# Sorting the edges by source on chip, and summing equal sources by a scan in place of joining products and accumulating scatters

## The reference

```python
def L0(x, src, dst, w):                       # first layer
    agg = segment_sum(x[src] * w[:, None], dst)
    out = leaky(x * agg @ W1 + b1) + leaky(agg @ W2 + b2)
    return out / norm(out)
def L1(x, src, dst, w):                       # second layer
    nbr = x[dst]                              # neighbours are now the destinations
    m = gelu(gelu(nbr @ W1p + b1p) @ W2p + b2p) * w[:, None]
    agg = segment_sum(m, src)                 # summed at the sources
    out = gelu(gelu([x, agg] @ W1u + b1u) @ W2u + b2u)
    return out / norm(out)
x = layernorm(x + L0(x, ...))
x = layernorm(x + L1(x, ...))
```

## Time and profile before

| What | us |
|---|---|
| median of 3 runs | 2925.66 (2924.0 to 2927.83) |
| the profiled execution's own time | 2925.36 |
| its span | 2923.6 |
| stage 1, to its last scatter's start | 1254.2 |
| stage 2, first gather to last scatter's start | 1258.3 to 2535.5 |
| stage 3 | 2539.0 to 2923.6 |
| busy: PE / DVE / ACT / POOL | 2133.4 / 2219.9 / 1060.2 / 2327.0 |
| moved by DMA | 516.39 MB |

### The profile page before, as it was taken

One profiled execution on the slowest core, in us unless ns is written; L12 is line 12 of the kernel. 1 busy time (PEld: TensorE's weight loads), 2 busy tenths in 40 slices (PEclk: granted clock), 3 DMA queues, 4 the chain that ended last, 5 costly groups with the idle time before them and its releaser, 6 DMA issues. The chain is left out here.

```text
span 2923.6 us, 40992 instructions
## 1 busy us (share of the span) xinstructions
PE 2133.4 (73%) x12594; PEld 1674.9 (57%) x12594; DVE 2219.9 (76%) x5824; ACT 1060.2 (36%) x1964; POOL 2327.0 (80%) x1770
## 2 busy tenths in 40 slices
PE   3036555555555553369999999999998999699997
PEld 3035555555555543347777777777776666466664
DVE  5069988888888886547788777777777777278998
ACT  0000000000000000035555555545554555289997
POOL 7777888888888888758878888888888887479998
PEclk8555555555555555579999999999999999699998
DMA  9889888888888767568777777777776776456664
GB/s 227 214 197 200 178 177 180 175 178 183 180 183 172 160 142 155 96 163 183 185 185 184 180 167 181 181 169 175 179 181 157 184 172 149 89 173 219 222 219 169
DMA packets 1035280, 516.39 MB, mean 177 GB/s; under 512 B 539713, under 2 KB 997489, under 8 KB 1035065
## 3 DMA queue, kind: packets, MB, share of 16 engines
q1 hardware_dynamic: 764616, 372.57, 48.1%
q0 software_dynamic: 143440, 76.97, 19.0%
q10 hardware_dynamic: 127008, 64.23, 7.6%
HBM read 269.84 MB, written 243.78 MB: 176 GB/s over the span
## 5 line engine op out<-in xcount | busy, mean ns | idle before, releaser
L304 PE MATMUL sums<-xg,weigh 128*128 128x64 f32 x1960 | 431.8, 416 | 518.2 <-ACT ms L327 350.9
L557 POOL DMA_INDIRECT state<-ms,sidx x391 | 621.5, 1590 | 147.4 <-issue 117.4
L304 PEld LDWEIGHTS sums<-xg,weigh 128*128 128x128 f32 x1960 | 417.6, 325 | 551.2 <-issue 474.9
L260 POOL DMA_INDIRECT table<-ms,sidx x391 | 615.7, 1575 | 136.1 <-issue 114.7
L372 DVE TENSOR_SCALAR weigh<-rowp,key,ew 128x128 f32<-128x128 f32 (+3 forms) x784 | 424.2, 604 | 162.8 <-PE rowp L292 155.4
L538 POOL DMA_INDIRECT box<-table,node_dst x391 | 385.8, 987 | 126.6 <-issue 111.2
L247 POOL DMA_INDIRECT xg<-in_x,node_src x391 | 380.8, 974 | 120.7 <-issue 107.1
L327 ACT ACTIVATE ms<-sums 128x256 f32<-128x256 f32 x98 | 37.6, 384 | 1137.9 <-DMA table<-ms,sidx 996.8
L378 DVE SCALAR_TENSOR_TENSOR seen<-rowp,key,earlier 128x128 f32<-128x128 f32 (+3 forms) x784 | 383.6, 546 | 0.0
L588 PE MATMUL z_p<-turned_s,wz 128*128 128x512 f32 x588 | 326.9, 639 | 22.7 <-ACT turned_s L670 21.0
L598 PE MATMUL o_p<-cenz,leaky 128*128 128x65 f32 x2352 | 302.1, 288 | 42.0 <-DVE leaky L758 41.9
(11 more groups left out here) (97 smaller groups left out, 3555.2 us busy)
## 6 DMA issues: line engine op xcount, KB each, us to landing
box<-table SPq DMA_DIRECT2D x97, 768.0 KB, 5.2
joins<-weigh ACTq DMA_DIRECT2D x98, 640.0 KB, 3.8
weigh_in<-joins SPq DMA_DIRECT2D x98, 640.0 KB, 7.1
table<-rows SPq DMA_DIRECT2D x97, 512.0 KB, 5.3
pair<-state SPq DMA_DIRECT2D x97, 512.0 KB, 4.0
xin<-in_x SPq DMA_DIRECT2D x97, 256.0 KB, 6.1
state<-y SPq DMA_DIRECT2D x97, 256.0 KB, 7.5
out<-y SPq DMA_DIRECT2D x97, 256.0 KB, 2.2
```

Source lines behind the costliest of these rows:

```text
L260: pool.indirect_dma_start(out=table[:, :], out_offset=bass.IndirectOffsetOnAxis(ap=sidx[0][:, i:i + 1], axis=0), in_=ms[k % MR][:, b, :], ...
L304: last = pe.matmul(sums[k % 2][:, a * D:(a + 1) * D], block_of(0, k, b)[:, a * P:(a + 1) * P], xg[:, k * WT + b, :], start=b == a, stop=b ...
L557: pool.indirect_dma_start(out=state[:, :], out_offset=bass.IndirectOffsetOnAxis(ap=sidx[1][:, at:at + 1], axis=0), in_=ms[k % SM][:, b, :] ...
```

## The change

What it does:

- The second call of `equal_rows` (sources as keys), `store_join`, the tensor `joins` and its load are gone.
- Beside stage 1 the 50,000 edges (padded to 65,536 as 128 x 512) are sorted by source with a bitonic network: 136 compare-and-swap steps, 16 changes of sign and 14 transpositions (steps over partitions are made after PE has turned the 128 x 512 arrays). A swap step is a comparison (256 elements a partition), a copy by ACT and two predicated copies by DVE (768 elements a partition each). 48 of these 166 entries stand in windows 0 to 3, the others, one or two a window, up to window 83.
- In stage 2 the gathers and scatters follow the sorted order. After the second GELU, DVE multiplies with the weights (`weight`) and sums runs of equal source by a scan along the free dimension (`sum_runs`), whose start is the last column of the window before. PE turns the sums back (`turn_back`), ACT copies them, and POOL scatters them plainly: only the last edge of a run goes to a real row, the others each to a row of their own that nobody reads. The sorted list lies as two halves in the two halves of the partitions; one accumulating scatter at the end (`add_seam`) adds the run that crosses from one to the other.
- The scatters no longer wait for the window before, and `leak` no longer waits for `begun`.
- The bias of the second product is added by ACT, and the two products with 128 columns and the one with `ones` become one with 256 columns.

```diff
@@ first_edges, DVE: one swap step
+ def compare(phase, bit, done, before_it):
+     wait(dve, arranged, done)
+     wait(dve, laid, 3 * before_it)
...
+     dve.tensor_tensor(compact(above[:, 0:COLS // 2]..., bit)[:, 0, :, :],
+                       keys[:, 0, :, 0, :], keys[:, 0, :, 1, :], ALU.is_gt).then_inc(compared, 1)
+ def swap(phase, bit):
...
+     dve.wait_ge(compared, n + 1)
+     dve.wait_ge(kept, n + 1)
+     dve.copy_predicated(both[:, :, :, 0, :], mask, both[:, :, :, 1, :]).then_inc(lowered, 1)
+     dve.wait_ge(lowered, n + 1)
+     dve.copy_predicated(both[:, :, :, 1, :], mask, compact(lower[:, :, :], bit)).then_inc(arranged, 1)
@@ first_edges, DVE: the order per window
- for n, k in order:
-     equal_rows(n, k)
-     if n == 0:
-         scatter_rows(k)
-         if k < NCH:
-             build(k)
+ for k in range(NWIN):
+     part = 0
+     for kind, phase, bit, done, before_it in sorting(k):
+         if kind == "sign":
+             change_sign(phase, done, before_it)
+         if kind == "swap":
+             compare(phase, bit, done, before_it)
+             if part == 0:
+                 weigh_rows(k)
+             if part == 1:
+                 count_rows(k)
+                 scatter_rows(k)
+             part += 1
+             swap(phase, bit)
...
+     if k < NCH:
+         build(k)
@@ first_edges, ACT
- def store_join(w):
-     act.wait_ge(weighed, turn[1, w] + 1)
-     act.dma_start(joins[w]..., weigh[1][w % 2]...).then_inc(joined[w % 2], 16)
+ def keep_lower(phase, bit, done, before_it):
+     wait(act, arranged, done)
+     wait(act, laid, 3 * before_it)
+     act.activation(compact(lower[:, :, :], bit), pairs(edges[:, :, :], bit)[:, :, :, 0, :], ACT.Copy).then_inc(kept, 1)
@@ second_edges, SP
- def load_join(i):
-     wait(sp, summed, i - SW + 1)
-     sp.dma_start(weigh[i % SW]..., joins[i]...).then_inc(joined[i % SW], 16)
+ def load_runs(i):
+     wait(sp, summed, i - SW + 1)
+     for h in range(2):
+         at = (HALF * h + 2 * i) * P
+         sp.dma_start(run[i % SW][h * D:(h + 1) * D, :, :],
+                      runs[:, at:at + 2 * P]....to_broadcast([D, 2, 2 * P])).then_inc(joined[i % SW], 16)
@@ second_edges, POOL
+ def scatter(k):
+     pool.wait_ge(taken, k + 1)
+     for b in range(min(WT, FILLED - k * WT)):
+         of = column_of(HALF * (b % 2) + 2 * k + b // 2)
+         pool.indirect_dma_start(out=state[:, :], out_offset=...sorted_sidx[:, of:of + 1]...,
+                                 in_=ms[k % SM][:, b, :], in_offset=None).then_inc(scattered[k % SM], 16)
@@ second_edges, PE
- pe.matmul(ffo[:, 0:WT * D], ones[:, :], bp2[:, :], start=True, stop=False)
- for q in range(2):
-     last = pe.matmul(ffo[:, q * P:(q + 1) * P], g1[:, q * P:(q + 1) * P], wp2[:, :], start=False, stop=q == 1)
+ pe.matmul(ffo[:, 0:2 * P], wp2[:, :], g1[:, :], start=True, stop=True).then_inc(mixed2, 1)
+ def turn_back(i):
+     pe.wait_ge(summed, i + 1)
+     wait(pe, taken, i)
+     for j in range(2):
+         last = pe.transpose(ffo[:, (2 + j) * P:(3 + j) * P], total[i % 2][:, j * P:(j + 1) * P], ident[:, :])
+     last.then_inc(turned_back, 1)
...
  of(t, 2, products, 2)
- of(t, 5, join)
  of(t, 4, turn_neighbours)
  of(t, 2, outputs, 0)
+ of(t, 5, turn_back)
  of(t, 2, outputs, 1)
@@ second_edges, ACT: take stands later
  of(t, 2, slope, 2)
- of(t, 5, take)
  of(t, 3, square_centred)
  of(t, 4, neighbours_in)
+ of(t, 5, take)
  of(t, 2, square)
@@ second_edges, DVE
- if q == 2:
-     wait(dve, begun, i - 4)
+ def weight(i):
+     dve.wait_ge(gelu2, i + 1)
+     dve.wait_ge(joined[i % SW], 32 * (i // SW + 1))
+     dve.tensor_tensor(g2[i % 2][:, :], g2[i % 2][:, :], run[i % SW][:, 1, :], ALU.mult).then_inc(weighted, 1)
+ def sum_runs(i):
+     dve.wait_ge(weighted, i + 1)
+     wait(dve, summed, i)
+     wait(dve, turned_back, i - 1)
+     dve.tensor_tensor_scan(total[i % 2][:, :], run[i % SW][:, 0, :], g2[i % 2][:, :],
+                            total[(i - 1) % 2][:, 2 * P - 1:2 * P] if i else 0.0, ALU.mult, ALU.add).then_inc(summed, 1)
...
  for t in range(ROUNDS):
+     of(t, 5, weight)
+     of(t, 5, sum_runs)
      of(t, 2, sum_outputs)
```

More of the change, by code:

```diff
@@ L56, in gnn_kernel, with column_of @@
     BEFORE_SCATTER = 3
-    SPAN = ((1, 2, 3, 4), tuple(b % JOIN + 1 for b in range(WT)))
-    JW = sum(SPAN[1])
+    SPAN = (1, 2, 3, 4)
+    HALF = TILES // 2
+    assert TILES % 8 == 0 and E < P * COLS and N < PAST_ALL
+    def column_of(tile):
+        return tile % 4 * P + tile // 4
     table = nc.dram_tensor("table", (3 * N + PAD, D), F32, kind="Internal").ap()
-    state = nc.dram_tensor("state", (2 * N + PAD, D), F32, kind="Internal").ap()
-    joins = nc.dram_tensor("joins", (NWIN, JW, P, P), F32, kind="Internal").ap()
+    state = nc.dram_tensor("state", (2 * N + 2 + P * COLS + P, D), F32, kind="Internal").ap()
+    runs = nc.dram_tensor("runs", (2, P * COLS), F32, kind="Internal").ap()
     table_rows = table[0:3 * N, :].rearrange("(n a) f -> n (a f)", a=3)
@@ L148, in first_edges @@
                 means = [means_p[:, s * G:(s + 1) * G] for s in range(2)]
+                spun_p = [pb(f"spun_p{s}", c) for s in range(2)]
+                above = pb("above", c)
                 prepared, masks, loaded, loaded2, keyed, padded, shifted = (sem(q) for q in (
@@ L176, in first_edges @@
                 assert NWIN >= NCH
-                order = [(0, 0)]
-                done = 0
-                for k in range(1, NWIN):
-                    order.append((0, k))
-                    while done < NWIN and (done <= k - 2 if k < BEFORE_SCATTER + 2 else done * NWIN <= k * (NWIN + 1)):
-                        order.append((1, done))
-                        done += 1
-                order += [(1, w) for w in range(done, NWIN)]
-                turn = {nk: q for q, nk in enumerate(order)}
@@ L187, in block_of @@
-                def block_of(n, k, b):
-                    at = sum(SPAN[n][0:b])
-                    return weigh[n][k % 2][:, at * P:(at + SPAN[n][b]) * P]
+                network = []
+                turned_now, changes, turns = False, 1, 0
+                for phase in range(1, PHASES + 1):
+                    for bit in range(phase - 1, -1, -1):
+                        if (bit >= LANES) != turned_now:
+                            turned_now = not turned_now
+                            network.append(("turn", phase, bit, changes, turns))
+                            turns += 1
+                        if bit == phase - 1:
+                            network.append(("sign", phase, bit, changes, turns))
+                            changes += 1
+                        network.append(("swap", phase, bit, changes, turns))
+                        changes += 1
@@ new lines, in first_edges, with sorting, upto @@
+                assert not turned_now
+                swap_number = {}
+                for kind, phase, bit, _, _ in network:
+                    if kind == "swap":
+                        swap_number[phase, bit] = len(swap_number)
+                FIRST, AT_ONCE, SORTED = 4, 12, 84
+                def sorting(k):
+                    def upto(r):
+                        if r <= FIRST:
+                            return min(AT_ONCE * r, len(network))
+                        return min(len(network), AT_ONCE * FIRST + -(-(len(network) - AT_ONCE * FIRST) * (r - FIRST) // (SORTED - FIRST)))
+                    return network[upto(k):upto(k + 1)]
@@ new lines, in turn_indices @@
+                        def turn_indices():
+                            pe.wait_ge(marked, 5)
+                            pe.wait_ge(laid, 3 * turns)
+                            for b in range(4):
+                                last = pe.transpose(spun_p[0][:, b * P:(b + 1) * P], ends[:, b * P:(b + 1) * P], ident[:, :])
+                            last.then_inc(spun_last, 1)
+                            for b in range(4):
+                                last = pe.transpose(spun_p[1][:, b * P:(b + 1) * P], edges[:, 1, b * P:(b + 1) * P], ident[:, :])
+                            last.then_inc(spun_last, 1)
+                            pe.transpose(above[:, COLS // 2:COLS // 2 + P], edges[:, 0, 3 * P:4 * P], ident[:, :]).then_inc(spun_last, 1)
@@ L344, in _ @@
                         take(NWIN - 1)
-                        for s in range(2):
-                            act.wait_ge(joined[s], 16 * lies(NWIN, s, 2))
                     @block.vector
```

339 lines of the change are left out of this document (219 added, 120 removed).

## The result

| | us |
|---|---|
| before, median of 4 runs | 2925.41 (2924.0 to 2927.83) |
| after, median of 4 runs | 3207.16 (3203.22 to 3207.82) |
| ratio | 1.0959, 95% interval 1.094 to 1.0978 |
| span before / after | 2923.6 / 3201.5 |

The change makes the kernel slower by 9.6%. The page of the kernel after, some of its lines: busy tenths of POOL and the granted clock in 40 slices, then groups (busy us, mean ns of one, idle before and its releaser).

A forecast was written before the change was run, and what follows sets the result against it. POOL was taken to bound both stages, with a circle through DVE, PE and ACT right behind it in stage 2. 2925.4 + 308 (stage 2) + 16 (stage 1) + 2 (end) = 3251 us, range 3060 to 3350.

The forecast's parts named there:

- POOL no longer paces, the circle does: Stage 2: plain scatters cut POOL's window from 12.5 to 10.2 us, so a dependency loop through DVE, PE and ACT paces.
- The circle, 15.72 us a round: Stage 2: chain from sum_outputs through leak, scan, turn and outputs to the next sum_outputs; 14.07 us, 15.72 with fallen clock.
- 97 x (15.72 - 12.55) = +308: Stage 2: 97 periods, each lengthened from 12.55 to 15.72 us, add 308 us.
- PE's `turn_back` waiting some 1.6 us each round: Stage 2, sign in the profile: between the halves of the outputs PE waits for DVE's total, some 1.6 us a round.
- The clock falls, in nearly every round: Stage 2: PE's idle gaps of about 2 and 1.6 us lower the granted clock; round 15.72 us against 14.07; chance 0.62.
- Stage 1, +16 us: Stage 1: the sort beside POOL's scatters adds 16 us, the middle between 0 and 32.
- the interference: Stage 1: DVE's sort work with both inputs in SBUF slows POOL's scatters, 0.11 us per 1.09 us of such work.
- removed: 0 us: Stage 1: the dropped comparisons, transposes and stores of joins were not on POOL, which sets the stage, so they save 0 us.
- The cover of DVE's work in stage 1: Stage 1: DVE's 9.4 us a window, sort included, fit under POOL's 11.4 us.
- The end, +2: End of stage 2: last three scatters 1.8 us cheaper, the seam's scatter and landing some 4 us more; +2 us.
- A held clock: Rival, stage 2: clock stays up, round 14.07 us, 3091 us in all, 3060 with the cheap scan; chance 0.15.
- The scan is no part of the circle: Rival, stage 2: scan ends with the first half of the outputs, round stays 11.96 us, 2886 us in all; chance 0.08.

The follow-up runs named there:

- e1: The changed kernel, with PE's turn_back behind the second half of the outputs and ACT's take behind its square; 3148.86 us, 1.0489 of the kernel before.
- e3: The changed kernel with useless PE products in both gaps, 8 before turn_neighbours and 6 before turn_back; 3090.95 us, 1.0298 of the kernel before.
- e7: The changed kernel with six useless PE products only between the halves of the outputs; 3377.16 us, 1.1226 of the kernel before.
- e5: The changed kernel with weights and scan right behind the third leak and 8 useless PE products before turn_neighbours; 2963.44 us, 0.9882 of the kernel before.
- e2: The changed kernel with DVE's weights and scan right behind the third leak, PE's list unchanged; 3296.57 us, 1.0982 of the kernel before.
- e4: The kernel before with stage 2's scatters plain, so adding of different windows' sums at one source is left out; 3301.35 us, 1.1007 of the kernel before.
- e6: The changed kernel with scan early, 8 useless PE products before turn_neighbours, and turn_back behind the outputs; 3016.15 us, 1.0028 of the kernel before.
- e9: The changed kernel without the sort, stage 2's scatters going to unread rows, only stage 1 compared; 3280.95 us, 1.09 of the kernel before.
- e8: The kernel before with stage 2's scatters plain and six useless PE products before the join; 3280.2 us, 1.0895 of the kernel before.

## Why the prediction was right, and where not

The forecast was 3251 us and 0.90 for slower; 3207 came. The span grew by 278 us where the parts gave 326 (308 + 16 + 2): 27 too much in stage 2 and 24 in stage 1, less 3 in small ones. The parts are:

- **POOL no longer paces, the circle does: right.** POOL's scatters are 0.97 us (0.98 taken from the earlier trace rows), and it waits for ACT's copy as written.
- **The circle, 15.72 us a round: right, and in part by luck.** The 93 rounds ahead of the stage's end take 15.70 us in the mean, most of them between 15.2 and 16.2. Its terms, as means over 57 rounds between 1600 and 2500 us: `sum_outputs` to the third `leak`'s end 8.54 (8.58 taken), from there to the scan's end 3.07 (3.12), hand-over 0.06 (0.18), turn 0.48 (0.59), second half of the outputs 2.66 (2.35), from there to `sum_outputs` 0.89 (0.90). The second half was 0.31 too cheap, and the others together 0.33 too dear. It was taken from the 4.70 us of the earlier trace rows; those outputs start at 1853.41, and the granted clock is 1.00 until 1854.00, so a part of them ran at the full clock. All 24 at the low clock take 5.38 us in e1. The scan is 0.75 us (0.74 taken), the weights 0.42. The Trainium skill's half throughput (DVE: opcode table, instruction layouts, handler registers and perf-mode slots, Datapath and trigger behaviour) agrees: 0.75 us stand beside 0.42 us for the multiplication of the same 256 elements.
- **The term that was mis-sized is the number of rounds.** "97 x (15.72 - 12.55) = +308" prices every period as a full round; the stage gave +282. The last four periods are shorter, 39 us in all where four full rounds are 63, as nothing more comes in behind them. The first scatters of the last two windows, 5.2 us apart:

```profile
2802.32 0.96 POOL L750 DMA_INDIRECT state<-ms,sorted_sidx  x1 [0.47 <-ACT ms L900]
...
2807.53 0.96 POOL L750 DMA_INDIRECT state<-ms,sorted_sidx  x1 [0.47 <-ACT ms L900]
```

  The 12.55 us of before is a mean over the same 97 periods, with its own last four at 9.4 to 9.6 us; the two were not of one kind.
- **"PE's `turn_back` waiting some 1.6 us each round": half of that.** Between 1600 and 2500 us it is 45.9 us over 58 rounds, 0.8 a round, because in many rounds the clock falls within the first half. The sum didn't use this wait, since the chain goes through DVE there, so nothing follows from it for the time.
- **The clock falls, in nearly every round: right**, and shown: filling both gaps restores it (e3), filling only the second does not (e7), filling only the first does with the scan early (e5).
- **Stage 1, +16 us: wrong in sign** (-8). The step that failed is the interference. A scatter of stage 1 takes 1,574 ns with the sort beside it and 1,575 before, although the predicated copies are 1.27 us in the mean (0.95 taken; half of them take about 1.0 us, the longest 1.9) and the sort is 404 us of DVE's time, 136 x (0.43 + 1.27 + 1.27), where 315 was taken. The Trainium skill's rule on the interface that POOL and DVE share (Advanced Engine Details and Errata, GPSIMD Details) shows no cost for these scatters here. The step "removed: 0 us" failed too: before, POOL waited for `ms` for some microseconds in stage 1, and these waits nearly go. Rows of the waits up to 1300 us, before and after (total us, times, longest):

```profile
POOL table L260 <- ACT ms L327: 12.8, 11, 2.8
...
POOL table L325 <- ACT ms L419: 1.3, 2, 0.7
```

  What of the change takes them away was not tried. On the other two chips the sign turns: the change reaches stage 2 at 1299.2 us on the second, before at 1282.7.
- **The cover of DVE's work in stage 1: right.** DVE is busy for 200.8 us of 250, 9.2 us a window (9.4 taken, 0.7 of it a wait and not work), under POOL's 11.4. The dearer copies did not make stage 1 DVE's on the first chip.
- **The end, +2: 3.3 measured.**
- **The rivals.** A held clock (3091 us forecast) was made by e3, at 3091 us on a chip on which the change takes 3358; on the first chip it would be lower by some share of that difference, so that the two numbers agree is chance. "The scan is no part of the circle" was given 2886 us and ruled out by the order; e5 makes the order so and is faster than before by 1.2%. It needs the filled gap too, which this rival did not have: its circle of 11.96 us was priced at full clock, and e2 shows 15.7.

## What to carry to other kernels

When work leaves TensorE, look at which wait it was filling: ten products that were "only a join" held the clock, and their going cost more (1.9 to 2.7 us a round) than the place of the scan that replaced them (1.3). Add up the chain of work and not the waits: where two engines run side by side, only the longer way counts, and slow products beside it are free until a cure makes them the longer way. So do not judge a cure by trying it alone: here two gave 0.5 and 2.7 us a round, and together 4.0. When a forecast multiplies a round by the number of windows, take both kernels' rounds in the same way, with or without the stage's end. And relieving the engine that paces a loop is no gain until the next circle is known: in e4 it was a loss.

## What the runs showed of the hardware that I had not expected

**Chips differ.** The kernel before takes 2925 us on one and 3001 to 3008 us on two others. Those two show idle times that no instruction explains: of ACT in stage 2 (in e5 and e6 in most rounds, up to 4.1 and 3.7 us between 1400 and 2500 us), of PE for 52 us or of ACT for 71 us at the start of stage 1; e1, on the second chip, has only one in stage 2, 15.3 us near its start. The few instruction fetches that the DMA view lists (74 in 900 us of e6, on two queues) come at other times than most of them: one starts within, or up to 1 us before, 22 of 70 such idle times. The cause is open.

**Relieving one engine can cost 10%** (e4, 3301 us against 3003), with nothing added. Its cause is open.

**The granted clock isn't the rate at which TensorE works in stage 1.** In e9 the profile grants 1.00 there, in the change 0.50, and the products take the same time. A stretch of stage 1 in e9 (busy columns as in the earlier trace rows), and PE in it:

```profile
800.00:1050.00 250.00, 117.77 (x528) 109.59 (x528) 127.53 (x360) 19.85 (x44) 203.03 (x153) 1.00 0.61 111
```

```profile
860.25 4.50 PE L358 MATMUL sums<-xg,weigh 128*128 128x64 f32 x20 [6.09 <-ACT ms L408]
```

The same of the change:

```profile
800.00:1050.00 250.00, 130.48 (x566) 118.33 (x567) 201.46 (x442) 46.45 (x81) 203.35 (x153) 0.50 0.60 109
```

```profile
863.20 4.50 PE L369 MATMUL sums<-xg,weigh 128*128 128x64 f32 x20 [5.92 <-ACT ms L419]
```

Twenty products take 4.50 us in both. Twenty of the same shape, the join of stage 2, take 4.11 us in the round of e8 shown above (0.55 granted over their time) and 2.34 us in its rounds at 1.00. The four transposes of the keys take 1.06 us in most windows of e9 at 1.00, 1.06 to 1.12 in the change at 0.50, and in a few windows of the change, at 1.00, 0.60. So in this stretch of e9 PE works as at the low level although the record says 1.00. The mean clock of a run is therefore not to be compared between kernels (e9's 0.829 in the table), and where the clock matters the duration of one known product is the surer reading.
